# A decoder layer on one core: SyncE's queue reordered, B and C loaded later, other halves by C on VectorE, pieces within slots reordered

## The reference

```python
xc, res = split(x @ W_in.T + b_in)                  # 256 -> 512 and 512
u = silu(causal_conv3(xc) + conv_b)
dlt, Bm, Cm = split(u @ W_x.T, [64, 80])            # B and C have 16 states
delta = softplus(dlt @ W_dt.T + b_dt)
h[t] = exp(delta[t] * A) * h[t-1] + delta[t] * Bm[t] * u[t]   # restarts every 64 steps
y = sum over states of h * Cm;  y = y * silu(res);  x = norm(x + y @ W_out.T + b_out)
x = norm(x + cross_attention(x, ctx))               # 16 heads of 16
x = norm(x + experts(x))                            # 8 experts, 704 wide, 32 tokens of a batch each
```

## Time and profile before

| What | Value |
|---|---|
| Median of 3 runs (lowest to highest) | 2763.23 us (2756.91 to 2768.07) |
| The profiled execution's own time | 2763.72 us |
| Its span, first to last instruction | 2761.9 us |
| Busy, share of the span: TensorE | 2428.5 us, 88% |
| VectorE | 2137.8 us, 77% |
| GpSimd | 2072.0 us, 75% |
| ScalarE | 1802.4 us, 65% |
| SyncE's queue: packets' time on the 16 DMA engines | 52.8% |

### The profile page before, as it was taken

One profiled execution on the slowest core, in us unless ns is written; L12 is line 12 of the kernel. 1 busy time (PEld: TensorE's weight loads), 2 busy tenths in 40 slices (PEclk: granted clock), 3 DMA queues, 4 the chain that ended last, 5 costly groups with the idle time before them and its releaser, 6 DMA issues. The chain is left out here.

```text
span 2761.9 us, 49852 instructions
## 1 busy us (share of the span) xinstructions
PE 2428.5 (88%) x14854; PEld 1665.1 (60%) x14854; DVE 2137.8 (77%) x3587; ACT 1802.4 (65%) x3972; POOL 2072.0 (75%) x967
## 2 busy tenths in 40 slices
PE   6678889888888898988888888989887879999997
PEld 4456666666666666666666666666665545555554
DVE  3788999999999999999999999999999732322333
ACT  3567888787888888877878787878887541111111
POOL 4999999999999999999999999999999500000000
PEclk8788999999999999999999999999999879999999
DMA  5365566666666666666666666666665342342221
GB/s 152 112 143 151 159 166 167 162 160 159 162 167 164 173 161 172 169 162 163 163 164 162 164 161 172 172 162 167 172 162 155 93 119 70 104 132 81 79 79 31
DMA packets 270171, 399.68 MB, mean 145 GB/s; under 512 B 115441, under 2 KB 190449, under 8 KB 265810
## 3 DMA queue, kind: packets, MB, share of 16 engines
q1 hardware_dynamic: 254546, 384.95, 52.8%
q10 hardware_dynamic: 15360, 11.55, 1.5%
HBM read 300.89 MB, written 94.37 MB: 143 GB/s over the span
## 5 line engine op out<-in xcount | busy, mean ns | idle before, releaser
L516 POOL TENSOR_TENSOR arena<-arena 128x1024 f32<-128x1024 f32 x512 | 1208.0, 2363 | 86.5 <-DMA arena<-w_dram 63.6
L615 ACT ACTIVATE dA_ps<-arena,a_neg 128x252 f32<-128x252 f32 x2048 | 868.8, 461 | 319.4 <-DVE dA_ps L819 172.6
L796 DVE TENSOR_TENSOR_SCAN arena<-dA_ps,arena 128x512 f32<-128x512 f32 x672 | 803.1, 1208 | 72.5 <-ACT dA_ps L615 34.5
L526 POOL TENSOR_TENSOR arena<-arena 128x1024 f32<-128x1024 f32 (+1 forms) x416 | 808.0, 1942 | 18.1 <-DVE arena L796 16.9
L796 DVE TENSOR_TENSOR_SCAN dA_ps<-dA_ps,arena 128x512 f32<-128x512 f32 x352 | 416.2, 1205 | 5.3 <-POOL arena L516 3.7
L925 PE MATMUL a_ps<-xT,w_conv 128*128 128x256 f32 x1536 | 365.5, 388 | 0.0
L867 DVE TENSOR_REDUCE mx<-s_ps 128x2 f32<-128x512 f32 x497 | 333.5, 671 | 22.8 <-PE s_ps L925 22.8
L925 PEld LDWEIGHTS a_ps<-xT,w_conv 128*128 128x128 f32 x1536 | 285.7, 192 | 53.4 <-issue 16.1
L925 PE MATMUL y_ps<-arena,sel 128*32 128x256 f32 x4096 | 257.1, 393 | 53.8 <-DVE m_rows L873 27.8
L673 ACT ACTIVATE probs<-st_ps 128x512 f32<-128x512 f32 x493 | 285.2, 578 | 25.7 <-PE st_ps L925 19.7
L925 PE MATMUL s_ps<-k_st,q_st 96*128 96x256 f32 x994 | 259.3, 343 | 41.8 <-DVE mx L867 28.5
(11 more groups left out here) (118 smaller groups left out, 3288.5 us busy)
## 6 DMA issues: line engine op xcount, KB each, us to landing
arena<-delta_dram SPq DMA_DIRECT2D x512, 128.0 KB, 2.8
arena<-w_dram SPq DMA_DIRECT2D x512, 128.0 KB, 3.2
arena<-bc_dram SPq DMA_DIRECT2D x128, 256.0 KB, 4.4
q_st<-q_parts_dram SPq DMA_DIRECT2D x512, 64.0 KB
k_st<-k_parts_dram SPq DMA_DIRECT2D x512, 64.0 KB
w_dram<-u SPq DMA_DIRECT2D x32, 512.0 KB, 2.8
delta_dram<-delta SPq DMA_DIRECT2D x32, 512.0 KB, 3.8
k_parts_dram<-parts SPq DMA_DIRECT2D x32, 512.0 KB, 3.8
```

The lines of the kernel that those rows point to most:

```text
L516: pool.tensor_tensor(dBu[:, n % NB], w_r[:, n // RP % 2, t % RP].unsqueeze(1).to_broadcast([P, QS, L]), bc_r[:, b.par, 0], ALU.mult).then_ ...
L526: pool.tensor_tensor(h[:, n % NH, states], h[:, n % NH, states], bc_r[:, b.par, 1, states], ALU.mult).then_inc(s_hC, 1)
L615: last = nc.scalar.activation(dA[n % NDA][:, q, :, 1:], delta_r[:, n // (2 * RP) % 2, t % RP].rearrange("p (c t) -> p c t", t=CH)[:, :, 1: ...
L796: nc.vector.tensor_tensor_scan(dst, decays, dBu[:, n % NB, 2 * half:2 * half + 2].rearrange("p q t -> p (q t)"), 0.0, ALU.mult, ALU.add).t ...
```

## The change

The list of VectorE's halves by C goes from eleven to ten; four are dropped and three are new. After it, tiles 5, 8 and 10 are wholly on VectorE and one half each of tiles 1, 2, 6 and 13; GpSimd has 9 full and 4 half pieces a batch in place of 8 and 5. All five lists of pieces are reordered, and some offsets change:

- SyncE: delta's store comes one slot earlier and ahead of w's; B and C are loaded in slot 14, directly before the first group of rows, in place of slot 11; the store of q goes to slot 12, ahead of the context load of slot 13; groups 1 and 2 of rows come one slot later, group 3 three slots earlier; the store of k and the token load come one slot earlier and so before group 1; x2's transposed store three slots earlier, the first expert's weights four slots earlier.
- ScalarE: softplus comes behind the first decay of its slot, the gate evacuations one slot earlier, the store of B and C one slot later.
- VectorE: a cleared half is cleared before the maximum of the scores, the residual of the first block comes behind the second scan of its slot, gating one slot earlier.
- TensorE: x2 is transposed one slot earlier, transposed maxima come behind the scores of their slot, and the transposes of heads before the projections of their slot.

```diff
@@ -42,7 +42,7 @@
 NB = 3
 NH = 7
 RP = 4
-HC_DVE = [(1, 0), (1, 1), (4, 1), (5, 0), (5, 1), (6, 1), (8, 0), (9, 1), (10, 0), (10, 1), (14, 1)]
+HC_DVE = [(1, 1), (2, 1), (5, 0), (5, 1), (6, 1), (8, 0), (8, 1), (10, 0), (10, 1), (13, 1)]
 HC_POOL = [t for t in range(NU) if (t, 0) not in HC_DVE or (t, 1) not in HC_DVE]
 NPROB = 5
 NX = 4
@@ -462,24 +462,24 @@
                 sp.dma_start(dst, x2T[:].rearrange("p k (e t) -> p (k e) t", t=EC)).then_inc(s_x2T_st, 16)
 
             run_steps([
+                (O_SP + 1, delta_store),
+                (O_XP + 5, bc_load),
+                (O_REP + 1, replicate(0)),
+                (O_REP + 10, replicate(3)),
+                (O_X2T + 7, load_columns),
+                (O_K + 4, store_parts(k_dram, s_k_hi, s_k_lo, s_k_dram)),
+                (0 + 1, load_x),
+                (O_LD + 23, load_tokens),
+                (O_LD + 13, load_expert(shared.load_w2)),
+                (O_SP + 1, w_store),
                 (O_K - 2, load_ctx),
-                (O_Q + 3, store_parts(q_dram, s_q_hi, s_q_lo, s_q_dram)),
-                (O_REP + 13, replicate(3)),
-                (O_LD + 11, load_expert(shared.load_w13)),
-                (O_LD + 14, load_expert(shared.load_w2)),
-                (O_LD + 23, load_tokens),
-                (O_K + 5, store_parts(k_dram, s_k_hi, s_k_lo, s_k_dram)),
-                (O_SP + 2, w_store),
-                (O_OUT, load_x_tok),
-                (0 + 1, load_x),
-                (O_SP + 2, delta_store),
-                (O_XP + 2, bc_load),
-                (O_REP + 1, replicate(0)),
-                (O_REP + 7, replicate(2)),
+                (O_REP + 8, replicate(2)),
+                (O_REP + 7, replicate(1)),
+                (O_LD + 7, load_expert(shared.load_w13)),
+                (O_OUT - 1, load_x_tok),
                 *[(O_LD + HG * gr - 2, load_stack(gr)) for gr in range(NG)],
-                (O_X2T + 3, load_columns),
-                (O_X2T + 3, store_x2T),
-                (O_REP + 6, replicate(1)),
+                (O_X2T, store_x2T),
+                (O_Q + 1, store_parts(q_dram, s_q_hi, s_q_lo, s_q_dram)),
             ], B)
             sp.wait_ge(s_q_dram, 16 * B)
             sp.wait_ge(s_k_dram, 16 * B)
@@ -529,8 +529,8 @@
 
             run_steps([
                 *[(O_SCAN + t - 1, dBu_piece(t)) for t in range(NU)],
+                *[(O_SCAN + t + 1, hC_piece(t)) for t in HC_POOL],
                 (O_SP + 2, w_piece),
-                *[(O_SCAN + t + 1, hC_piece(t)) for t in HC_POOL],
             ], B)
 
         @block.scalar
@@ -730,25 +730,25 @@
                 return piece
 
             run_steps([
-                (O_SP + 1, softplus),
                 (O_V + 1, v_evac),
                 (O_SILU, silu),
-                *[(O_GATE + 4 * half + 2, later_gate_evac(half)) for half in range(2)],
+                (O_K + 1, high(s_k_mm, s_k_hi, s_q_dram, 1)),
+                *[(O_SCAN + t - 1, decay(t, 0)) for t in range(NU)],
+                (O_N2 + 3, store_x2),
+                *[(O_GATE + 4 * half + 1, later_gate_evac(half)) for half in range(2)],
+                (O_ONT - 1, onT_evac),
+                (O_SP + 1, softplus),
+                *[(O_CONV + 4 * half + 3, conv_evac(half)) for half in range(2)],
+                *[(O_MT + HG * gr + 2, max_store(gr)) for gr in range(NG)],
+                (O_Q + 1, high(s_q_mm, s_q_hi, s_k_dram, 0)),
+                *[(O_MT + HG * gr + 1, max_high(gr)) for gr in range(NG)],
+                (O_XP + 1, xp_evac),
+                *[(O_MT + HG * gr + 3, max_load(gr)) for gr in range(NG)],
+                (O_XP + 2, bc_store),
+                (O_N2, norm(1, s_mv2, s_ln2, s_x2)),
+                *[(O_PV + HG * gr + 1, oT_evac(gr)) for gr in range(NG)],
+                *[(O_SCAN + t - 1, decay(t, 1)) for t in range(NU)],
                 (O_SP + 2, first_gate),
-                (O_K + 1, high(s_k_mm, s_k_hi, s_q_dram, 1)),
-                (O_N2 + 3, store_x2),
-                *[(O_SCAN + t - 1, decay(t, 0)) for t in range(NU)],
-                *[(O_MT + HG * gr + 2, max_store(gr)) for gr in range(NG)],
-                *[(O_MT + HG * gr + 3, max_load(gr)) for gr in range(NG)],
-                (O_XP + 1, xp_evac),
-                *[(O_MT + HG * gr + 1, max_high(gr)) for gr in range(NG)],
-                (O_N2, norm(1, s_mv2, s_ln2, s_x2)),
-                *[(O_CONV + 4 * half + 3, conv_evac(half)) for half in range(2)],
-                (O_ONT - 1, onT_evac),
-                *[(O_PV + HG * gr + 1, oT_evac(gr)) for gr in range(NG)],
-                (O_XP + 1, bc_store),
-                (O_Q + 1, high(s_q_mm, s_q_hi, s_k_dram, 0)),
-                *[(O_SCAN + t - 1, decay(t, 1)) for t in range(NU)],
                 *[(O_E + hd, softmax_exp(hd)) for hd in range(H)],
                 (O_X2T, x2T_evac),
                 (O_N1 - 3, norm(0, s_mv1, s_ln1, s_x1)),
@@ -901,19 +901,19 @@
                 nc.vector.tensor_copy(x1T[:], a_ps[:]).then_inc(s_x1T, 1)
 
             run_steps([
+                *[(O_SCAN + t, scan(t, 0)) for t in range(NU)],
+                (O_K + 1, low(s_k_hi, s_k_lo)),
+                *[(O_ON + HG * gr + 1, head_norm(gr)) for gr in range(NG)],
+                (O_X1T + 1, x1T_evac),
+                (O_OF + 1, residual(1, s_of_mm, a_ps, s_r2, s_st2, s_mv2, s_ln2, s_x1, TT)),
+                *[(O_SCAN + t, scan(t, 1)) for t in range(NU)],
                 (O_SP + 2, first_w),
-                *[(O_SCAN + t, scan(t, 0)) for t in range(NU)],
-                (O_OF + 1, residual(1, s_of_mm, a_ps, s_r2, s_st2, s_mv2, s_ln2, s_x1, TT)),
-                (O_X1T + 1, x1T_evac),
-                (O_K + 1, low(s_k_hi, s_k_lo)),
                 (O_OUT + 1, residual(0, s_out_mm, a_ps, s_r1, s_st1, s_mv1, s_ln1, s_xtok, 16)),
-                *[(O_ON + HG * gr + 1, head_norm(gr)) for gr in range(NG)],
-                *[(O_SCAN + t, scan(t, 1)) for t in range(NU)],
                 *[(O_SCAN + t, hC_piece(t, half)) for t, half in HC_DVE],
+                *[(O_SCAN + t, clear_starts(t, half)) for t, half in HC_DVE],
                 *[(O_S + hd + 1, row_max(hd)) for hd in range(H)],
-                *[(O_SCAN + 4 * m + 6, gating(m)) for m in range(ND)],
-                *[(O_SCAN + t, clear_starts(t, half)) for t, half in HC_DVE],
                 (O_Q + 1, low(s_q_hi, s_q_lo)),
+                *[(O_SCAN + 4 * m + 5, gating(m)) for m in range(ND)],
                 *[(O_MT + HG * gr + 1, max_low(gr)) for gr in range(NG)],
             ], B)
 
@@ -1166,23 +1166,23 @@
             run_steps([
                 *[(O_E + hd, scores_T(hd)) for hd in range(H)],
                 *[(O_PV + HG * gr, pv(gr)) for gr in range(NG)],
+                *[(O_V, v_proj(tt)) for tt in range(TT)],
+                *[(O_DT, dt_proj(m)) for m in range(ND)],
+                (O_X2T - 1, transpose(x_of, s_x2, TT, s_x2T_mm, s_x2T, bank_a, a_ps)),
+                *[(O_OF, attn_out(tt)) for tt in range(TT)],
                 *[(O_CONV + 2 * m, conv(m)) for m in range(ND)],
+                (O_X1T, transpose(x_of, s_x1, TT, s_x1T_mm, s_x1T, bank_a, a_ps)),
+                (O_XP, x_proj),
                 *[(O_GATE + 4 * (m // 2), later_gate(m)) for m in range(ND)],
+                *[(O_OUT, out_proj(tt)) for tt in range(TT)],
+                (O_ONT - 2, transpose(lambda b: on, s_on, NG, s_onT_mm, s_onT, bank_a, a_ps)),
+                *[(O_ON + HG * gr, head_transpose(gr)) for gr in range(NG)],
+                *[(O_K, k_proj(m)) for m in range(KD)],
+                *[(O_Q, q_proj(m)) for m in range(KD)],
                 (O_SP + 1, first_gate),
-                (O_X1T, transpose(x_of, s_x1, TT, s_x1T_mm, s_x1T, bank_a, a_ps)),
-                *[(O_DT, dt_proj(m)) for m in range(ND)],
-                *[(O_V, v_proj(tt)) for tt in range(TT)],
-                *[(O_OF, attn_out(tt)) for tt in range(TT)],
-                *[(O_OUT, out_proj(tt)) for tt in range(TT)],
-                *[(O_K, k_proj(m)) for m in range(KD)],
-                (O_ONT - 2, transpose(lambda b: on, s_on, NG, s_onT_mm, s_onT, bank_a, a_ps)),
-                *[(O_Q, q_proj(m)) for m in range(KD)],
-                (O_X2T, transpose(x_of, s_x2, TT, s_x2T_mm, s_x2T, bank_a, a_ps)),
-                *[(O_ON + HG * gr, head_transpose(gr)) for gr in range(NG)],
-                (O_XP, x_proj),
-                *[(O_MT + HG * gr, max_transpose(gr)) for gr in range(NG)],
                 *[(O_S + hd, scores(hd)) for hd in range(H)],
                 *[(O_SCAN + 4 * m + 4, state_sum(m)) for m in range(ND)],
+                *[(O_MT + HG * gr, max_transpose(gr)) for gr in range(NG)],
             ], B)
 
 
```

## The result

The changed kernel took 2966.84 us (median of 4 runs, 2958.14 to 2982.74), the kernel before beside it 2760.07: a ratio of **1.0761, 95% interval 1.0726 to 1.0797**. It is slower, as forecast, but by 207 us and not by 77, and lies above the range.

A forecast was written before the change was run, and what follows sets the result against it. A loop through the context load bounds the batches: D 55.1 + C 14.2 = 69.3 us, above GpSimd's 65.03; +2.6 us times 30 = +77 on 2763.72 gives 2841 us, ends cancelling. Range 2775 to 2935 us.

The forecast's parts named there:

- C: Stretch of a batch from the context load to the next batch's first product; forecast to go from 10.3 to 14.2 us.
- the copies' 4.4 us: Four copies of B and C, 1.05 MB, now ahead of the rows in SyncE's queue: 4.4 us a batch added.
- The rivals with quicker or hidden copies: Quicker: B and C's copies cost 2.7 us, 2789 us, chance 0.05. Hidden: covered behind w's store, 2797 us, chance 0.13.
- D: Rest of a batch's period, from first product to the next context load; forecast to go from 56.4 to 55.1 us.
- the ends: Start and seam outside the batch loop: -3 us at the start, +3 at the seam, forecast to cancel.
- Softplus behind a decay: ScalarE's softplus falls behind one more decay: 0 to 0.9 us on w.
- The forecast's loop: First product to context load (D), then to the next first product (C): period 69.3 us, +2.6 us a batch.
- GpSimd's added half: GpSimd takes one more half by C: +1.09 us a batch, raising its floor to 65.03 us.
- the first rival: Only the added half shows: copies covered, GpSimd's extra work adds 34 us, 2797 us; chance 0.13.
- GpSimd's waits for VectorE would nearly vanish: Sign that the forecast is right: GpSimd's waits for VectorE, 22.0 + 16.9 us before, nearly gone.
- The worse rival: D does not shrink, VectorE waits for state sums, second group stalls: period 72.9 us, +185, 2949 us; chance 0.10.
- The second group of rows: Store of k and token load now precede it in SyncE's queue: costed at nothing, up to 3 us without cover.

The follow-up runs named there:

- that wait filled: Changed kernel with four unused products of constants on TensorE where it waits for softplus: 2911.07 us, ratio 1.0549.
- both waits are filled: Changed kernel with four unused products in TensorE's softplus wait and six before each batch's first scores: 2888.59 us, ratio 1.0475.

## Why the prediction was wrong

**C was right.** 14.2 us were forecast, the mean is 13.9 (before 10.5); the copies' 4.4 us hold, and moving them behind w takes most of it away. The rivals with quicker or hidden copies fall with it.

**D was the step that failed.** It was to shrink from 56.4 to 55.1 us and grew to 59.1: 4 us a batch, times 30, is 120 us, nearly all of the 126 between 2841 and 2967. (C came out 0.3 lower than forecast, -9 us, and the ends added 14.) Its two parts, as means over batches 5 to 29 (they add up to D within 0.2):

- From w's end to the context load 55.1 - 52.3 = 2.8 us were implied, and 5.4 came. The projection of V, and q's before its store, were taken at the durations of the earlier trace rows, whatever stands in front of them. Softplus behind a decay was costed "0 to 0.9 us on w" and the transposes of heads before the projections were not costed at all; together they make TensorE wait 2.1 us, and behind it q is projected at the lower clock in 21 of the 32 batches, V in 9 of them. With that wait filled the time is 3.1 us, as in the batches where both run at full clock: the rest of the step was right. The batch of the earlier trace rows was one of the quick ones, too: 4.1 us, where the mean of the kernel before is 4.8.
- From the first product to w's end 52.3 us were forecast, and 53.9 came (51.5 before). The halves alone give 52.5, and GpSimd's own work in it grows from 50.5 to 52.5, so their +2.2 was about right. Of the other 1.4 us, 0.6 goes when both waits are filled (53.3); the 0.8 us that remain were not settled.

The forecast's loop left TensorE's clock out: it moved waits of TensorE about as if a wait cost its own length. With both waits filled D is 55.9, 0.8 from the forecast.

**GpSimd's added half** gave the first rival its 34 us, by the Trainium skill's rule of the busiest engine (Perfetto Trace Analysis, Identifying the Most-Contended Engine). The run of the halves alone disagrees: -6 us, although GpSimd was the busiest engine of the batches (97.8 of 100 us in the earlier trace rows). The forecast that GpSimd's waits for VectorE would nearly vanish holds in that run (6.9 us) and not in the changed kernel (43.2), where VectorE itself waits longer for decays (92.5 us, 34.5 before).

**The worse rival** came nearest in time, 2949 us, and its period of 72.9 us meets the measured 72.96, but by luck, since its mechanism is another: VectorE does wait more, for scores above all (98.1 us, 22.8 before), yet with both of TensorE's waits filled that wait is 21.5 us and D is nearly back, without an edit to VectorE; and the second group of rows did not stall.

**The second group of rows** was costed at nothing, rightly: over batches 5 to 29 GpSimd waits 6.4 us a batch at the first product and 0.1 at the fifth. **The ends** were to cancel. The start gave -1.9 for -3, but from the last w to the end it is 16.2 us more, where +3 was taken and 5.8 was the bound. With SyncE's list of before it is 670.5 us (682.3 in the changed kernel, 666.1 before), so some 12 of the 16 us hang on SyncE's list; which part of it is the first expert's weights was not tried.

**The range** fell short at the top because its upper ends took VectorE's waits and the second group of rows, and no case had TensorE below full speed, although the row gives the duration of the work on which the loop turned, and the price of doing it at the other clock could be estimated from there as up to 1.99 us more for V, as much for q; in the batch shown it was 1.79 each.

## What to carry to other kernels

Before a transfer or a piece is moved, list the waits of TensorE that get longer by it, and take into the range the case that the work behind it runs at half the clock; here products in one wait of 2.1 us, which did not make softplus come sooner, brought the context load 2.3 us forward. An engine with a high busy share isn't therefore the one without slack: add a known amount of work to each candidate, at the place in question, and see which period grows. Where parts of a change act on the same wait, they don't add, so take them out one at a time and also together.

## What was not expected of the hardware

- Work added to an engine that waits made the kernel faster: eight unused products in each of 30 batches took 91 us off, and in the stretches shown the granted clock behind the wait went from 0.63 to 1.00.
- Short waits matter. In the changed kernel's batch shown, a wait of 2.12 us was followed by 10 us at a mean granted clock of 0.51. In the kernel before, in TensorE's timeline of one batch, q behind a wait of 1.18 us ran at the upper level, while V, behind a second one of 1.14 us, had already slowed down:

```profile
1092.82 0.46 PE L925 MATMUL a_ps<-bias 4*128 4x512 f32 x1 [1.18 <-ACT delta L605]
1093.22 1.99 PE L925 MATMUL a_ps<-x1T,w_q 128*128 128x256 f32 x8
...
1096.80 0.47 PE L925 MATMUL st_ps<-q_st,k_st 96*128 96x256 f32 x2 [1.14 <-ACT probs L673]
...
1097.63 2.86 PE L925 MATMUL f_ps<-w_v,ctxT 128*128 128x256 f32 x8
```

- A single line on SyncE's queue, one that moved 1.05 MB by three slots, cost 235 us in a kernel of 2758; the period grew by 7.0 us (73.78 - 66.74) for 4.4 us of copies.
